# Attention of a two-layer transformer: scores copied out of PSUM, the tail of a head issued behind the next head's scores, transposed blocks copied by two engines

## What is computed

```python
att = jnp.einsum('bkgid,bkjd->bkgij', q, k) / scale
att = jnp.where(causal, att, -jnp.inf)
att = jax.nn.softmax(att, axis=-1)
y = jnp.einsum('bkgij,bkjd->bkgid', att, v)
y = y.transpose(0, 3, 1, 2, 4).reshape(b, t, E)
y = y @ Wo + bo
```

## Time and profile before

| | us |
|---|---|
| runs of the kernel before | 22,925.41 and 23,493.06, median 23,209.24 |
| profiled execution | 22,513.0 |
| its span on the slowest core (core 0) | 22,511.5 |
| spans of the eight cores | 22,197.2 to 22,511.5 |
| TensorE, VectorE, ScalarE busy | 15,488.1 (69%), 6,374.5 (28%), 2,335.1 (10%) |
| attention of layer 0, of layer 1 | 4,791 and 2,511 |

### The profile page before, as it was taken

One profiled execution on the slowest core, in us unless ns is written; L12 is line 12 of the kernel. 1 busy time (PEld: TensorE's weight loads), 2 busy tenths in 40 slices (PEclk: granted clock), 3 DMA queues, 4 the chain that ended last, 5 costly groups with the idle time before them and its releaser, 6 DMA issues.

```text
span 22511.5 us, 190991 instructions; the slowest of 8 cores (22197.2 to 22511.5 us)
## 1 busy us (share of the span) xinstructions
PE 15488.1 (69%) x68311; PEld 6742.3 (30%) x69360; DVE 6374.5 (28%) x15592; ACT 2335.1 (10%) x3370; POOL 494.8 (2%) x522
## 2 busy tenths in 40 slices
PE   6433333333568998999956853444559999899999
PEld 2111111111233443444422321222224444344443
DVE  4344444544211111111123224444321111111111
ACT  1111111111000000000011011111010000000000
POOL 0000000000000000000000000000000000000000
PEclk9655555555789999998866765555668899998988
DMA  2100000001245445443331100001243334443333
GB/s 53 26 3 2 1 2 1 1 2 29 87 93 80 62 69 101 72 74 62 62 91 35 26 32 4 3 3 34 77 93 62 64 64 81 99 82 62 63 61 71
DMA packets 810912, 1122.61 MB, mean 50 GB/s; under 512 B 22929, under 2 KB 678930, under 8 KB 783122
## 3 DMA queue, kind: packets, MB, share of 16 engines
q0 software_dynamic: 737920, 793.00, 22.2%
q1 hardware_dynamic: 72082, 317.32, 3.9%
HBM read 1772.98 MB, written 130.24 MB: 85 GB/s over the span
## 4 chain that ended last, share of the span: by engine, by line
PE 60%; DVE 19%; DMA 8%; issue 6%; ACT 5%; SPq 1%; DVEq 1%; POOL 0%; ACTq 0%; POOLq 0%
PE PS L999 17%; PE PA L1069 10%; PE PC L1069 10%; PE PS L1033 6%; DVE CCR L700 4%; DVE ST L676 4%; DVE ST L685 4%; ACT CCR L680 4%; PE PS L663 4%; PE PBb L695 3%; DMA WCb<-wd 3%; PE PC L708 3%; PE PA L1154 1%; DMA WCb<-w 1%; PE PC L1154 1%
## 5 line engine op out<-in xcount | busy, mean ns | idle before, releaser
L695 PE MATMUL PBb<-IDT,CCR 128*128 128x128 bf16 x3456 | 910.2, 263 | 4178.0 <-ACT CCR L680 2468.4
L999 PE MATMUL PS<-R,FWAb 128*128 128x512 bf16 x13297 | 3138.3, 397 | 407.8 <-DMA R<-xnC 151.7
L1069 PE MATMUL PA<-WCb,R 128*128 128x512 bf16 x9297 | 2374.6, 405 | 290.1 <-DMA WCb<-wd 210.3
L1069 PE MATMUL PC<-WCb,R 128*128 128x512 bf16 x9331 | 2353.4, 401 | 13.8 <-issue 0.2
L1078 DVE SCALAR_TENSOR_TENSOR ACCv<-PA,CMB,ACCv 128x512 f32<-128x512 f32 x864 | 649.0, 751 | 4968.1 <-PE PA L1069 4811.8
L999 PEld LDWEIGHTS PS<-R,FWAb 128*128 128x128 bf16 x13568 | 1367.8, 101 | 2169.4 <-issue 1085.4
L695 PEld LDWEIGHTS PBb<-IDT,CCR 128*128 128x128 bf16 x3456 | 361.6, 105 | 5130.2 <-issue 5130.2
L1013 ACT ACTIVATE R<-PS 128x512 bf16<-128x512 f32 x1188 | 709.4, 597 | 10127.3 <-PE PS L999 10127.2
L1033 PE MATMUL PS<-R,FWBb 128*128 128x512 bf16 x6899 | 1589.6, 390 | 8.4
L1069 PEld LDWEIGHTS PA<-WCb,R 128*128 128x128 bf16 x9504 | 972.9, 103 | 1565.0 <-issue 888.1
L1069 PEld LDWEIGHTS PC<-WCb,R 128*128 128x128 bf16 x9504 | 970.2, 102 | 1254.4 <-issue 557.3
(11 more groups left out here) (186 smaller groups left out, 9082.7 us busy)
## 6 DMA issues: line engine op xcount, KB each, us to landing
WCb<-w POOLq DMA_DIRECT2D x32, 5632.0 KB, 35.3
FWAb<-w POOLq DMA_DIRECT2D x64, 1536.0 KB, 15.8
WCb<-wd POOLq DMA_DIRECT2D x16, 5632.0 KB, 39.7
FWAb<-wg POOLq DMA_DIRECT2D x48, 1536.0 KB, 14.5
FWBb<-wu POOLq DMA_DIRECT2D x48, 1536.0 KB, 14.3
FWBb<-w POOLq DMA_DIRECT2D x32, 1536.0 KB, 15.4
FWBb<-w POOLq DMA_DIRECT2D x32, 1024.0 KB, 9.3
TSa<-x SPq DMA_DIRECT2D x24, 1024.0 KB, 5.2
```

What stands on the lines that cost most here:

```text
L695: (lambda j, pp, ATTs: lambda t: t.transpose([self.PBb, self.PDB][pp][:, 0:128], ATTs[:, j * 128:(j + 1) * 128], self.IDT[:, :]))(j, pp, A ...
L999: (lambda k, m, n, ps, gslot, wid: lambda t: t.matmul(ps, gslot[:, k * wid + m * 128:k * wid + (m + 1) * 128], R1[:, k * 1024 + n * 512:k ...
L1069: (lambda k, mtq, nn, psd, nslab: lambda t: t.matmul(psd[:, :], R1[:, GOF + k * 1024 + mtq * 128:GOF + k * 1024 + mtq * 128 + 128], WC[:, ...
```

## The change

It has four parts, all in `attention` and a new function `_attn_tail`.

1. ScalarE copies the masked scores from PS to a float32 buffer in SBUF, SCF (two buffers by the parity of h, laid over WA and WB), and the exp reads SCF instead of PS. The next head's scores wait for this copy (`ps_guard`), not for the exp. The copy waits for mask add and maximum, the exp for the copy.
2. The tail of a head (transposes, their copies, A·V, evacuation) is kept in `pend` and emitted one head later: behind the next head's scores, ahead of the next head's mask add. The last head of a row tile has its tail emitted at once.
3. The copies of transposed blocks go to VectorE and ScalarE in turn (`cp_flip` counts over all heads). On ScalarE it is a plain copy.
4. The statistics (c0 to c2 in ST) have two sets by the parity of h; A·V waits for the last copy of either engine.

The diff, cut to its core; the removed loops of transposes, A·V and evacuation come back in `_attn_tail`, with the lines shown changed:

```diff
@@ -299,6 +299,8 @@
...
+        self.SCF = [at("SCFa", [128, 2048], F32, offset=WW_OFF),
+                    at("SCFb", [128, 2048], F32, offset=WW_OFF + 16384)]
...
@@ -634,18 +636,25 @@
...
+        ps_guard = []
+        self._attg = [None, None]
+        scf_guard = [None, None]
+        pc_guard = None
+        cp_flip = [0]
+        pend = None
...
+                SCFs = self.SCF[hp]
+                c0 = ST[:, 4 * hp:4 * hp + 1]
+                c1 = ST[:, 4 * hp + 1:4 * hp + 2]
+                c2 = ST[:, 4 * hp + 2:4 * hp + 3]
...
-                wl0 = list(t_kv) + ([exp_guard] if exp_guard else [])
+                wl0 = list(t_kv) + list(ps_guard)
...
+                if pend is not None:
+                    pc_guard = self._attn_tail(**pend)
...
                 t_mx = em.emit("vector",
-                               (lambda W: lambda v: v.reduce_max(
-                                   ST[:, 0:1], self.PS[:, 0:W], axis=AX.X, negate=True))(W),
-                               wait=[t_mk], inc=self.ve)
-                t_exp = em.emit("scalar",
-                                (lambda W, ATTs: lambda s: s.activation(
-                                    ATTs[:, 0:W], self.PS[:, 0:W], AF.Exp, bias=ST[:, 0:1]))(W, ATTs),
-                                wait=[t_mx], inc=self.se)
-                exp_guard = t_exp
+                               (lambda W, c0: lambda v: v.reduce_max(
+                                   c0, self.PS[:, 0:W], axis=AX.X, negate=True))(W, c0),
+                               wait=[t_mk] + ([scf_guard[hp]] if scf_guard[hp] else []), inc=self.ve)
+                wl_ev = [t_mk, t_mx]
+                if scf_guard[hp]:
+                    wl_ev.append(scf_guard[hp])
+                t_ev = em.emit("scalar",
+                               (lambda W, SCFs: lambda s: s.activation(
+                                   SCFs[:, 0:W], self.PS[:, 0:W], AF.Copy))(W, SCFs),
+                               wait=wl_ev, inc=self.se)
+                ps_guard = [t_ev]
+                wl_ex = [t_mx, t_ev]
+                if self._attg[hp]:
+                    wl_ex.append(self._attg[hp])
+                t_ex = em.emit("scalar",
+                               (lambda W, ATTs, SCFs, c0: lambda s: s.activation(
+                                   ATTs[:, 0:W], SCFs[:, 0:W], AF.Exp, bias=c0))(W, ATTs, SCFs, c0),
+                               wait=wl_ex, inc=self.se)
+                scf_guard[hp] = t_ex
...
-                t_rc = em.emit("vector", lambda v: v.reciprocal(ST[:, 2:3], ST[:, 1:2]),
+                               (lambda W, ATTs, c1: lambda v: v.reduce_sum(
+                                   c1, ATTs[:, 0:W], axis=AX.X))(W, ATTs, c1),
+                               wait=[t_ex], inc=self.ve)
+                t_rc = em.emit("vector", (lambda c1, c2: lambda v: v.reciprocal(c2, c1))(c1, c2),
...
-                t_cp = None
...
-                    t_cp = em.emit("vector",
...
-                                   wait=[t_tp], inc=self.ve)
...
-                wl = [t_cp] + ([pc_guard] if pc_guard else [])
...
-                t_ev = em.emit("scalar",
-                               (lambda h, ysl, dh: lambda s: s.activation(
-                                   ysl[:, h * dh:(h + 1) * dh], self.PC[:, 0:dh],
-                                   AF.Copy, scale=ST[:, 2:3]))(h, ysl, dh),
-                               wait=wl2, inc=self.se)
-                pc_guard = t_ev
-                ev_last = t_ev
+                pend = dict(i=i, h=h, hp=hp, ATTs=ATTs, ATTTs=ATTTs, t_ex=t_ex, t_rc=t_rc,
+                            vcol=vcol, dh=dh, c2=c2, ysl=ysl, R1=R1,
+                            y_wait=(ysl_tok[i % 2] if h == 0 else None), cp_flip=cp_flip,
+                            pc_guard_in=pc_guard)
+                if h == nheads - 1:
+                    pc_guard = self._attn_tail(**pend)
+                    pend = None
...
             t_y = em.dma("sync", d["y_hbm"][i * 128:(i + 1) * 128, :], ysl[:, :],
-                         self.dS[i % 2], wait=[ev_last])
+                         self.dS[i % 2], wait=[self._last_yevac])
...
+    def _attn_tail(self, i, h, hp, ATTs, ATTTs, t_ex, t_rc, vcol, dh, c2, ysl, R1,
+                   y_wait, cp_flip, pc_guard_in):
+        em = self.em
...
+        cp_last = {}
...
+        for j in range(i + 1):
+            pp = j % 2
+            g = self._tt_guard[pp]
+            t_tp = em.emit("tensor",
...
+                           wait=[t_ex, self.static_tok] + ([g] if g else []), inc=self.pe)
+            att_done = t_tp
+            eng = "vector" if (cp_flip[0] % 2 == 0) else "scalar"
+            cp_flip[0] += 1
+            t_cp = em.emit(eng,
+                           (lambda j, pp, ATTTs: lambda e: e.tensor_copy(
+                               ATTTs[:, j * 128:(j + 1) * 128],
+                               [self.PBb, self.PDB][pp][:, 0:128]))(j, pp, ATTTs)
+                           if eng == "vector" else
+                           (lambda j, pp, ATTTs: lambda e: e.copy(
+                               ATTTs[:, j * 128:(j + 1) * 128],
+                               [self.PBb, self.PDB][pp][:, 0:128]))(j, pp, ATTTs),
+                           wait=[t_tp], inc=self.ve if eng == "vector" else self.se)
+            self._tt_guard[pp] = t_cp
+            cp_last[eng] = t_cp
+        self._attg[hp] = att_done
+        wl = list(cp_last.values()) + ([pc_guard_in] if pc_guard_in else [])
...
+        wl2 = [t_av, t_rc]
+        if y_wait:
+            wl2.append(y_wait)
+        t_evy = em.emit("scalar",
+                        (lambda h, ysl, dh, c2: lambda s: s.activation(
+                            ysl[:, h * dh:(h + 1) * dh], self.PC[:, 0:dh],
+                            AF.Copy, scale=c2))(h, ysl, dh, c2),
+                        wait=wl2, inc=self.se)
+        self._last_yevac = t_evy
```

More of the change, by code:

```diff
@@ L691, in attention @@
[L691 to L698, removed]
-                    t_cp = em.emit("vector",
-                                   (lambda j, pp, ATTTs: lambda v: v.tensor_copy(
-                                       ATTTs[:, j * 128:(j + 1) * 128],
-                                       [self.PBb, self.PDB][pp][:, 0:128]))(j, pp, ATTTs),
-                                   wait=[t_tp], inc=self.ve)
-                    self._tt_guard[pp] = t_cp
@@ L705, in attention @@
-                wl = [t_cp] + ([pc_guard] if pc_guard else [])
[L706 to L711, removed]
-                                       start=(j == 0), stop=(j == i)))(j, i, ATTTs, vcol, dh),
-                                   wait=wl if j == 0 else (),
-                                   inc=self.pe if j == i else None)
@@ L725, in attention @@
+                if h == nheads - 1:
+                    pc_guard = self._attn_tail(**pend)
+                    pend = None
+                    if True:
+                        pass
             t_y = em.dma("sync", d["y_hbm"][i * 128:(i + 1) * 128, :], ysl[:, :],
-                         self.dS[i % 2], wait=[ev_last])
+                         self.dS[i % 2], wait=[self._last_yevac])
             ysl_tok[i % 2] = t_y
+    def _attn_tail(self, i, h, hp, ATTs, ATTTs, t_ex, t_rc, vcol, dh, c2, ysl, R1,
+                   y_wait, cp_flip, pc_guard_in):
+        em = self.em
+        t_cp = None
+        cp_last = {}
+        att_done = None
+        for j in range(i + 1):
+            pp = j % 2
+            g = self._tt_guard[pp]
+            t_tp = em.emit("tensor",
+                           (lambda j, pp, ATTs: lambda t: t.transpose(
+                               [self.PBb, self.PDB][pp][:, 0:128],
+                               ATTs[:, j * 128:(j + 1) * 128], self.IDT[:, :]))(j, pp, ATTs),
+                           wait=[t_ex, self.static_tok] + ([g] if g else []), inc=self.pe)
[15 more added lines that the diff above has]
+        wl = list(cp_last.values()) + ([pc_guard_in] if pc_guard_in else [])
+        for j in range(i + 1):
+            t_av = em.emit("tensor",
+                           (lambda j, i, ATTTs, vcol, dh: lambda t: t.matmul(
+                               self.PC[:, 0:dh],
+                               ATTTs[:, j * 128:(j + 1) * 128],
+                               R1[:, vcol(j):vcol(j) + dh],
+                               start=(j == 0), stop=(j == i)))(j, i, ATTTs, vcol, dh),
+                           wait=wl if j == 0 else (),
+                           inc=self.pe if j == i else None)
+        wl2 = [t_av, t_rc]
[7 more added lines that the diff above has]
+        self._last_yevac = t_evy
+        return t_evy
```

9 lines of the change are left out of this document (removed).

## The result

The changed kernel took 21,981.79 us in the median of 11 runs (21,136.05 to 22,863.20), the kernel before 22,849.98 us in the median of 10 (22,373.28 to 23,493.06). The medians lie 868 us or 3.8% apart. The ratio is 0.9375 with a 95% interval of 0.9165 to 0.9584, so the kernel is faster, by over twice the 2.7% that the sum gave.

What follows compares the result with a forecast made beforehand. Attention was taken as bound by a chain of waits per head, 768 heads; terms from -1,492 and +827 to small ones summed to -613 us, so 23,209 - 610 = 22,600 us, range 21,800 to 23,100.

Steps and rivals of the forecast that it cites:

- the sum: All predicted terms in the two attention phases added up: -613 us, 2.7% of the profiled execution of 22,513 us.
- has no part in what makes those differ: Whole kernel: the change only takes microseconds off attention, not affecting what separates the two runs shown (22,925 and 23,493 us).
- Scores and A·V leave the chain: Attention heads: next scores run during the exp, A·V beside the next mask add and maximum; -1,492 us.
- the +35 for gaps: VectorE in attention: small gaps of 0.03 to 0.05 us before mask adds that now follow a copy; +35 us.
- The PS copy enters it: ScalarE between maximum and exp: unhidden copy +827 us, dearer exp from SBUF +25, wait between copy and exp +77.
- The rival of an overlapping pair: ScalarE: the exp's start-up hides behind the PS copy, 131 us better, -744 us in all; chance 0.12.
- Half of the copies on ScalarE: Copy phase: sharing doesn't shorten it; VectorE only gains the last PDB copy or a spare copy; about -185 us.
- ScalarE the last in layer 1: Layer 1 attention: PS copy waits behind A·V's evacuation in ScalarE's queue, late by 0.48 us at n = 16; +80 us.
- Dearer ScalarE copies: Copy phase: 128x128 copies cost 367 ns and delay VectorE's transposes; -465 us, or -390 with a longer wait; chance 0.24.
- a slower kernel by the same loop: Copy phase: ScalarE round trips hold up VectorE's transposes; 2% slower, 23,670 us, needs some 750 ns a copy; chance 0.05.
- a halved copy phase: Copy phase: the split halves it, as if VectorE's work were its bound; -1,530 us, 21,680 us; chance 0.04.
- a missing overlap: Attention: scores or A·V stay exposed because a guard releases late; time moves under 150 us, 23,150 us; chance 0.05.

Runs made afterwards that it cites:

- rerun: The changed kernel unedited, run again beside the kernel before on the same chip; attention 6,543 us, whole median 22,151 us.
- att_cut: The kernel before with only an eighth of the heads in both attention phases; attention 916 us, whole median 16,933 us.
- att_twice: The kernel before with each attention phase done twice in a row; attention 14,622 us, whole median 29,829 us.
- defer_only: The kernel before with only the tail issued one head late and two sets of statistics; attention 5,784 us, whole median 21,386 us.
- no_scf: The changed kernel without the copy from PS to SCF, exp reading PS; attention 5,696 us, whole median 21,533 us.
- no_split: The changed kernel with all copies of transposed blocks on VectorE; attention 6,683 us, whole median 22,304 us.
- batch_sum: no_scf plus up to four transposes per PSUM bank and copy, and the row sum from the exp's accumulator; attention 4,480 us, whole median 20,075 us.

## Why the prediction was right or wrong

**The step that failed** is the last one of the sum: from microseconds in attention to a time and a comparison of the kernel as a whole. I wrote that the change "has no part in what makes those differ", and as far as rerun, att_cut and att_twice show, that held. But I took the level of the two runs shown as given, 3% above the profiled execution, and didn't ask what the difference of levels was. The profile of before had the answer: stretches of the dense phases with a granted clock of 0.82 and 0.96 for the same work, 3,675 and 4,234 matmuls in 1,000 us. With 14,450 to 16,500 us outside attention by die, the luck of an execution is up to 2,000 us, three times the effect forecast, and a ratio of a few executions can lie 3% beside the change. From 15,100 us outside attention for both, the change alone would give (6,545 + 15,100) / (7,299 + 15,100) = 0.966; from the least of each, (6,545 + 14,420) / (7,299 + 14,458) = 0.964. The measured ratio is 0.9375, and its interval doesn't reach either. So of the 6.25% some 3.4 to 3.6 are the change, and the rest is the clock of the executions compared. What makes the chip grant that clock in one execution and not in another stays open. The range for the time, 21,800 to 23,100, does hold the median of 21,982, and for this reason alone: it was drawn across both levels. The 618 us between the forecast of 22,600 and that median are 359 from the level (the two runs shown had a median of 23,209, all ten 22,850), 141 from attention and, but for rounding, 114 by which the medians differ more than attention does.

**Scores and A·V leave the chain, -1,492:** right. defer_only alone measured -1,515; with the +35 for gaps, which belongs to it, the sum had -1,457.

**The PS copy enters it, +827, +25, and +77 for the wait:** right in mechanism and nearly in size. The copy reads 1.88 us at 2,048 columns, the exp 2.00, the gap 0.08 where I took 0.10; removing it gave 847 us (no_scf) and 899 (defer_only against no_split), against 913 by the corrected gap and 929 in the sum. The rival of an overlapping pair fell with the 0.08: the exp waits for the copy's result and stays behind it, while the PS copy, which doesn't wait for the evacuation of A·V, starts 0.10 us before that ends (14554.44).

**Half of the copies on ScalarE, -185:** the mechanism was right (VectorE's loop stays at 0.74 us a pair, 5.20 us for seven from 4985.53 to 4990.73; the phase isn't halved), and the split is worth 140 us in the change and 18 without the deferral. The copy reads 266 ns, not 277, and ScalarE starts 0.10 us after the transpose, not 0.15, so its loop is 0.77 us (transposes at 4986.03 and 4986.80) and not 0.84. The 0.15 was taken from A·V, whose end is modelled. That kept ScalarE's lateness small.

**ScalarE the last in layer 1, +80, and the gaps of +35:** these two terms were mis-sized, and with them most of the sum's error. The faster loop lets A·V start at 5.87 us behind VectorE's first copy in place of 6.34, and the evacuation and the PS copy overlap by 0.10 us. ScalarE is still the last in layer 1, as forecast, but the term is 40 us and not 80, and its course over n was wrong: I had 0.1 us at n = 2 rising to 0.48 at n = 16, and the rows have 0.2 at n = 4 and 0.04 at n = 16. And a mask add behind a copy doesn't wait 0.03 to 0.05 us but starts 0.08 us before the copy's end, which is 768 x 0.08 = 61 us gained instead of 35 lost. -613 - 40 - 35 - 61 = -749, against -754 measured. The 0.08 us between PS copy and exp (-15) and the 13 us by which ScalarE is late in layer 0, which the sum didn't have, nearly cancel. The experiments give the same difference in three parts: deferral -1,515 where the sum had -1,457, PS copy +899 where it had +929, split -140 where it had -85 (-185 + 80 + 20). They add up to -756.

**The rivals.** Dearer ScalarE copies, a slower kernel by the same loop, an overlapping pair, a halved copy phase and a missing overlap each have a row against them above: copies at 0.266 us, a gap of 0.08, VectorE's copies 0.74 apart, and no wait for scores. The case that decided, two kernels compared at unlike clocks, was not among the rivals. It is no rival to the mechanism, but it was one to the number.

## What to carry to other kernels

Where a chain of waits goes round once per head, write down which work of the next round could stand in each engine's queue ahead of the present round's tail; moving instructions in the queue alone was worth 1,515 us here, and a copy added to free the buffer early cost 850 to 900, because the work that it released had room already. A phase of transpose, copy, transpose was bound here by its round trips: a second engine for the copies brought 18 us by itself. So put more into one trip (four blocks a bank) first; batch_sum did that together with the accumulator, and what each brought isn't known. And before forecasting the time of a kernel on all cores, compare the granted clock of the same dense stretch on different cores and in different stretches: if it isn't the same, the change is forecast as a difference in the stretch that it touches, and its ratio only with the clock's spread around it.

## What the runs showed of the chip that I had not expected

- Two dies in one execution of one program can differ by 885 us of 21,941: one at 0.97 to 1.00 of the clock in the dense phases, the other at 0.81 to 0.82 for stretches of a millisecond. Over all kernels the time outside attention went from 14,420 to 16,488 us by die. What picks the die and the stretch stays open; one sixteenth of the attention left the least time outside it within 10 us.
- An instruction on VectorE that doesn't depend on the one before it starts 0.08 us before that one ends (copy, then mask add), while a dependent one on ScalarE starts 0.08 us after it (PS copy, then exp), and on VectorE 0.10 after (mask add, then maximum).
- VectorE's copy of a transposed block from PSUM takes 0.22 us for 128 columns and 0.42 for 512, so a quarter of the instructions cost half of the time per column, apart from the round trips saved.
